# One Gelu per hidden tile, its high half copied in SBUF, and four passes written out

## The reference, cut to what matters

```python
h = gelu(einsum('td,edh->eth', xf, W1) + b1[:, None, :])          # layer 0: 8 experts, 1024 hidden
expert_out = einsum('eth,ehd->etd', h, W2) + b2[:, None, :]
...
o0 = gelu(xf @ e0_up.T) @ e0_down.T                               # layer 1: 4 experts, 512 hidden
o1 = silu(xf @ e1_w1.T) * (xf @ e1_w2.T) @ e1_down.T
o2 = gelu(gelu(gelu(xf @ e2_l1.T) @ e2_l2.T) @ e2_l3.T) @ e2_l4.T
o3 = gelu(gelu(xf @ e3_down.T) @ e3_up.T) @ e3_out.T
```

## Time and profile before

| | |
|---|---|
| median of three runs | 3157.91 us (3155.34 to 3163.25) |
| the profiled execution: its own time | 3164.51 us |
| its span, first to last instruction | 3162.7 us |
| TensorE busy | 2791.1 us (88%) |
| ScalarE busy | 1819.6 us (58%) |
| VectorE busy | 1643.0 us (52%) |
| GpSimd busy | 1428.1 us (45%) |
| mean granted TensorE clock | 0.963 of full speed |
| DMA | 235.92 MB, mean 75 GB/s |

### The profile page before, as it was taken

The page is one execution under the profiler, slowest core; times in us unless marked ns, Lnnn a source line. Parts: engine busy times, 40 slices in busy tenths (PEclk is TensorE's granted clock), DMA queues, the critical chain, the costliest instruction groups (busy, mean ns, idle before and its releaser), DMA issues. The chain is left out here.

```text
span 3162.7 us, 58694 instructions
## 1 busy us (share of the span) xinstructions
PE 2791.1 (88%) x22208; PEld 1862.8 (59%) x22208; DVE 1643.0 (52%) x3100; ACT 1819.6 (58%) x2899; POOL 1428.1 (45%) x1358
## 2 busy tenths in 40 slices
PE   3899958998999989998989898989898998987878
PEld 1555535665665666566656675667565765653555
DVE  5776735436446444644365436634563465446452
ACT  3666635555765666565565565565556655654634
POOL 5666523443454435443544454444444443453334
PEclk8999979999999999999999999999999999999999
DMA  1000028621121212121212122212222121210002
GB/s 62 21 27 13 20 74 309 239 102 66 54 92 68 78 68 93 67 82 61 96 68 82 65 81 73 89 64 74 80 82 73 66 74 61 73 41 22 24 23 76
DMA packets 59719, 235.92 MB, mean 75 GB/s; under 512 B 6560, under 2 KB 25024, under 8 KB 40640
## 3 DMA queue, kind: packets, MB, share of 16 engines
q1 hardware_dynamic: 57920, 228.13, 20.6%
q0 software_dynamic: 1536, 4.20, 0.5%
HBM read 200.57 MB, written 31.72 MB: 73 GB/s over the span
## 5 line engine op out<-in xcount | busy, mean ns | idle before, releaser
L1408 POOL TENSOR_TENSOR c_lo<-c_g,c_hi 128x512 bf16<-128x512 f32 x720 | 887.6, 1240 | 1347.0 <-ACT c_hi L1570 1222.3
L2247 PE MATMUL c_up<-c_xT,c_ring 128*128 128x512 bf16 x3072 | 750.8, 384 | 69.3 <-ACT c_hi L1570 56.0
L2264 PE MATMUL c_down<-c_ring,c_hi 128*128 128x256 bf16 x4096 | 715.4, 275 | 0.0
L1569 ACT ACTIVATE c_g<-c_up,b 128x512 f32<-128x512 f32 x512 | 352.9, 689 | 491.1 <-PE c_up L2247 487.1
L2264 PE MATMUL c_down<-c_ring,c_lo 128*128 128x256 bf16 x2048 | 563.3, 275 | 0.0
L2247 PEld LDWEIGHTS c_up<-c_xT,c_ring 128*128 128x128 bf16 x3072 | 295.7, 99 | 367.4 <-ACT c_hi L1570 67.5
L2264 PEld LDWEIGHTS c_down<-c_ring,c_hi 128*128 128x128 bf16 x4096 | 398.3, 99 | 106.0 <-issue 2.2
L1570 ACT ACTIVATE c_hi<-c_up,b 128x512 bf16<-128x512 f32 x512 | 350.9, 685 | 0.0
L1836 DVE CAST c_room<-c_room 128x384 bf16<-128x384 f32 x256 | 128.2, 530 | 403.7 <-PE c_front L2159 307.8
L1569 ACT ACTIVATE c_g<-c_up 128x512 f32<-128x512 f32 x176 | 105.5, 600 | 295.1 <-PE c_up L2000 289.0
L2264 PEld LDWEIGHTS c_down<-c_ring,c_lo 128*128 128x128 bf16 x2048 | 202.1, 99 | 25.0
(11 more groups left out here) (339 smaller groups left out, 5438.4 us busy)
## 6 DMA issues: line engine op xcount, KB each, us to landing
c_ring<-kept_dense SPq DMA_DIRECT2D x112, 1024.0 KB, 4.8
c_ring<-kept_experts SPq DMA_DIRECT2D x63, 512.0 KB, 3.4
c_room<-in_WB SPq DMA_DIRECT2D x16, 1024.0 KB, 7.0
kept_dense<-c_ring SPq DMA_DIRECT2D x16, 1024.0 KB, 4.8
c_ring<-kept_experts SPq DMA_DIRECT2D x28, 384.0 KB, 3.4
kept_experts<-c_room SPq DMA_DIRECT2D x9, 512.0 KB, 3.8
c_xT<-kept_xT SPq DMA_DIRECT2D x8, 512.0 KB, 5.2
out<-h SPq DMA_DIRECT2D x8, 512.0 KB, 6.6
```

The costliest lines, as they stand in the source:

```text
L1408: pool.tensor_tensor(lo14[:, a, :], g[:, h % 4, :], hi14[:, a, :], ALU.subtract).then_inc(lo_ready.sem, 1)
L1569: act.activation(g[:, h % 4, :], ub[n % 2][:, :], ACT.Gelu, bias=bias)
L2247: last = pe.matmul(ub[n % 2][:, :], r[:, wp, o + q * P:o + (q + 1) * P], xT[:, xp, q, :], start=(m == 0 and q == 0), stop=(m == 2 and q == ...
L2264: m = pe.matmul(bank, (hi14, lo14)[xp][:, a, s * P:(s + 1) * P], r[:, wp, o + KC * P:o + CHUNK], start=False, stop=(k == HC0 - 1 and n == ...
```

## The change

Gelu is made once per U or I unit, into `g`, and raises a new semaphore `g_ready`. ScalarE waits for its own `g_ready` and copies `g` to `hi14` with the conversion to bf16, which raises `hi_ready` as before. `bank_free` waits for `g_ready` of the unit two before, no longer for `hi_ready`. A table `plan.gelu` numbers the units that make a Gelu. Both loops over passes 3 to 6 become Python loops, so that the four passes stand one after the other in the instruction stream of each engine, with constants in the waits.

```diff
@@ Plan.__init__
-        self.up, self.bank_user, self.hid, self.group, self.gate = {}, [], {}, {}, {}
+        self.up, self.bank_user, self.hid, self.group, self.gate, self.gelu = {}, [], {}, {}, {}, {}
         n_hid = n_group = 0
         for u in self.units:
             if u[0] in "UI":
                 self.up[u] = len(self.bank_user)
                 self.bank_user.append(u)
+                self.gelu[u] = len(self.gelu)
@@ phase_bc
+        g_ready = Both(x.enter_context(nc.semaphore("c_g_ready")), NB, len(PLAN_C.gelu))
@@ run
-            with eng.Fori(3, TILES - 1) as i:
+            for i in range(3, TILES - 1):
                 go(ORDER_BC, dense(i, PLAN_BC, PLAN_BC), front(i - 1), gates(i - 2))
@@ block.sync
-            with sp.Fori(3, TILES - 1) as i:
+            for i in range(3, TILES - 1):
                 streamed(i, PLAN_BC, PLAN_BC)
@@ block.scalar, dense
-                    act.activation(g[:, h % 4, :], ub[n % 2][:, :], ACT.Gelu, bias=bias)
-                    act.activation(hi14[:, a, :], ub[n % 2][:, :], ACT.Gelu, bias=bias).then_inc(hi_ready.sem, 1)
+                    act.activation(g[:, h % 4, :], ub[n % 2][:, :], ACT.Gelu, bias=bias).then_inc(g_ready.sem, 1)
+                    act.wait_ge(g_ready.sem, g_ready.at(i, plan.gelu[u] + 1))
+                    act.activation(hi14[:, a, :], g[:, h % 4, :], ACT.Copy).then_inc(hi_ready.sem, 1)
@@ block.tensor, bank_free
                         if v[0] == "G":
                             pe.wait_ge(gate_sl.sem, gate_sl.at(first_tile(i), plan.gate[v] + 1))
                         else:
-                            pe.wait_ge(hi_ready.sem, hi_ready.at(i, plan.hid[v] + 1))
+                            pe.wait_ge(g_ready.sem, g_ready.at(i, plan.gelu[v] + 1))
                     elif before is not None and before.dense:
-                        pe.wait_ge(hi_ready.sem, hi_ready.at(i, n - 1))
+                        pe.wait_ge(g_ready.sem, g_ready.at(i, n - 1))
```

## The result

The changed kernel took 3141.75 us, the median of five runs (3139.86 to 3145.17), against 3157.19 us for the kernel before in five runs: ratio 0.995, interval 0.9937 to 0.9963. That is 15.4 us faster where 37.9 were forecast. The time lies inside the range, the sign is right, and the likeliest case is not what happened: the figure is that of the rival in which only the written-out passes count (3142 us).

A forecast was written before the change was run, and what follows sets the result against it. TensorE, busy 88% of the span, was taken to set the time except in its waits. Terms -28.6 + 3.9 + 7.5 - 16.0 - 4 = -37.2 us from 3157.9 gave 3120.7, say 3120 us; range 3097 to 3144.

The forecast's parts named there:

- only the written-out passes count: Rival: TensorE's gain from the early bank is waited away at VectorE or ScalarE's front work; 3142 us, chance 0.13.
- The passes written out: Passes 3 to 6: without the loop's branch back and registers computed ahead of waits, 16.0 us gained.
- The bank's release: TensorE's waits for ScalarE's second Gelu: bank free earlier, 0.55 us for each of 52 waits, 28.6 us gained.
- what of it is spent again: TensorE's wait for VectorE's `h`: absorbs one wait of 0.55 us in each of seven passes, 3.9 us lost.
- The longer pair: ScalarE's Gelu plus copy: holds ScalarE 89 us longer, mostly hidden; 7.5 us charged where TensorE waits for front work.
- The rival in which it costs 89 us: Slower, by ScalarE: the longer pair lands on the path in the attention part; 3202 us at worst, chance 0.09.
- The clock: TensorE's half-speed stretches after waits: waits of 2.7 us become 2.2 us, 4 us gained.

The follow-up runs named there:

- e1: Kernel before with only the loops over passes 3 to 6 written out, no Gelu edit: 3140.38 us, ratio 0.995.
- e3: Changed kernel, but a bank is free only when hi is ready, after the copy: 3152.31 us, ratio 0.9988 to the kernel before.
- e5: Changed kernel with VectorE's recurrence cut short (reciprocal left out, one product and sum on 32 of 512 columns): 3091.96 us, ratio 0.9764.
- e7: Changed kernel with four VectorE instructions per half tile of the recurrence reading one operand in PSUM: 3108.82 us, ratio 0.982.
- e10: Changed kernel with the Gelu edit in the 512 U units alone, I units as before: 3135.08 us, ratio 0.9928.
- e2: Kernel before with only the Gelu edit, loops kept: 3158.3 us, ratio 1.0002.
- e6: e1 with four VectorE instructions per half tile of the recurrence reading one operand in PSUM: 3118.77 us, ratio 0.9844 to the kernel before.
- e12: e7 with one number of the work order changed and the Gelu edit in U units alone: 3081.95 us, ratio 0.9757 to the kernel before.

## Why the prediction came out half wrong

**The passes written out** were sized right: 16.0 forecast, 17.0 measured by e1. By the table, whose means differ by 18.2 us, 11.9 us are the rest and 6.3 the clock, so a part of what the earlier trace rows showed as the loop's price was its slow stretches.

**The bank's release** does what was said, wait by wait: 0.56 us at the place of the earlier trace rows, and 26.1 us less of the bank's waits between e3 and the changed kernel (104.9 to 78.8), against 28.6 forecast. Against the kernel before it is 17.8 us, since the longer pair had first made these waits longer (97.8 in e1, 104.9 in e3), and the 16 waits of line 2003 gave only 1.8 of it, where 0.55 us each was counted. **The step that failed is what of it is spent again: "I count one wait of 0.55 us in each of seven passes".** The wait for `h` took back just that: 24.5 + 6.8 to 27.8 + 7.1 us, 3.6 us in all. But the same passes have further meetings with VectorE and ScalarE that showed no wait or a small one in the earlier trace rows, and these filled: `c_xhi` 10.3 to 19.6 us, `c_qs` 13.6 to 17.8 us. With 17.1 us returned, 9.0 of the 26.1 remain, and e3 and the changed kernel differ by 10.6. With the recurrence shortened (e5, e7) the edit was worth 10.7 and 7.5 us at full clock in place of 2.4. I had looked for the waits that exist, not for the chain that stands just behind TensorE and has no slack.

**The longer pair** costs ScalarE what was said (hi is ready 1.35 us after the Gelu's start in a U unit and 1.26 us in an I unit, medians; 1.37 and 1.28 forecast). Before, the medians were 1.27 and 1.09, so ScalarE is held 73 us longer and not 89. On the path it costs 11.9 us where 7.5 were taken, if e3 is taken for it; by the table 7.0 us of that are delay and 7.1 clock (from the means, which differ by 14.1 us). The size of the delay was right, for a reason that I can't claim: the charge was a rounded estimate. The rival in which it costs 89 us was far off.

**The clock** has the wrong sign, and is the second step that failed. "I take 4 us for the kernel" was a gain; the Gelu edit loses 5.8 us by it, and the whole change gains 0.5 (109.8 to 109.3). The case for it was "Waits of 2.7 us become 2.2 us". The slow row stands behind a wait of 2.46 us, some 12 us into the pass. In the changed kernel it did become 2.20 us, and the clock still fell behind it in four of five passes. The wait of 2.7 us, at 218 us of the pass, was 2.77 us in e1 and 2.85 in the changed kernel; it became 2.19 in e10, where the I unit ahead of it is left alone. The loss came with the longer pair: e3 already loses 7.1 us more than e1 on the same chip, and with the early release it is 1.3 us less (110.6 and 109.3). In e3 the stretch at 176 us can account for it. What accounts for it in the changed kernel stays open; the head of the pass is slow four times of five in e3 too, but in e1 twice and in e2 only once.

**The rivals.** *Only the written-out passes count* gave 3142 us and was given 0.13. It had the mechanism, a gain that is waited away at VectorE and at the front, and the objection raised against it, that such waits come once a pass and the bank's seven times, was the error: a chain need be met only once a pass to take all that was gained since the last meeting. In the table's terms the Gelu edit is -9.4 us (release) + 7.0 us (pair) = -2.4 us at full clock and +5.8 us by the clock, each uncertain by 1 to 3 us, +3.4 us in the means and +1.4 us in the medians, against -21.2 us forecast. Of the 24.6 us between forecast and means, some 15 are the release's gain given back and some 10 the clock.

## What to carry to other kernels

A wait that shrinks by the forecast amount is not a gain until it is known who is met next. Follow the gain down the pass to the next engine with a serial chain, also where the profile shows no wait there, because a chain that is just on time has no line in the list of waits; the distance between the chain's start and its consumer (56.1 and 57.4 us here) shows it. And compare mean granted clocks over all runs before a small difference is put down to the edit: here an edit that saved 2.4 to 10.7 us at full clock was mostly paid back in slow stretches. Make such an edit only in the units where it shortens waits: in the U units it took 19.2 us from them and was kept, in the I units 2.2 us and brought nothing.

## What the runs showed of the hardware

- A product or sum on VectorE with two f32 operands of 512 columns in SBUF took 0.69 us alone, and also when it began 0.10 us ahead of GpSimd's subtraction (e1). Where GpSimd had begun first it took mostly 1.39 to 1.65 us. With one operand in PSUM it took 0.69 us beside GpSimd in all 16 cases of line 1723 (e6). With four instructions of the recurrence changed so, and nothing left out, the kernel got 1.1% faster (e6 against e1: ratios 0.9844 and 0.995).
- A copy on ScalarE behind its own Gelu's semaphore waits 0.03 us, but the overlap of two neighbours (0.11 us) is lost with it, and a pair is then as long as TensorE's unit: in the changed kernel two Gelus of a run of I units start at 1893.20 and 1894.49, 1.29 us apart, and TensorE's products for them at 1893.00 and 1894.29, also 1.29 us. ScalarE no longer catches up in such a run.
- The branch back of the loop over a pass stalled TensorE for 2.97 us, 2.81 and 2.42 us, and no stall of that kind stands at the heads of the written-out passes.
- The same stretch of a pass can have either clock from pass to pass, and one kernel's runs spread in the mean clock by 0.001 (e10) to 0.006 (e12, 0.969 to 0.975), which is 3 to 19 us of its time. Chips differ as well: the kernel before lost 110 us to the clock on one and 119 on another, with the rest of its time alike to 3 us.
